# An attention block with normalization and a feed-forward layer: the second softmax's probabilities turned by transfers and 32x32 blocks

## The chip, the cores and the metric

The kernel runs on one core of one Trainium2 chip. The metric is the device time of one execution in microseconds (us), the median of several runs.

## What is computed

Two sequences of 1024 tokens with 256 features pass a normalization with a learned modulation, an attention with **two softmaxes**, and a feed-forward layer. The first softmax, over the first 128 features of queries and keys, gives a context whose tanh corrects the queries of the second.

```python
SCALE = 1.0 / float(np.sqrt(HEAD_DIM))                   # 1/4
qkv = hidden_states @ c_attn_w + c_attn_b
Q, K, V = jnp.split(qkv, 3, axis=2)
attn_scores = jnp.einsum('bse,bte->bst', Q, K) * SCALE
Q_cam, K_cam, V_cam = (Q[:, :, :D_K], K[:, :, :D_K], V[:, :, :D_K])      # D_K = 128
base_A = softmax(jnp.einsum('bsd,btd->bst', Q_cam, K_cam) * SCALE)
layer_weight = sigmoid(cam_w0[0] + cam_w1[0] * LAYER_DEPTH)
cam_ctx = jnp.einsum('bst,btd->bsd', base_A, V_cam)
cam_bias = jnp.einsum('bsd,btd->bst', jnp.tanh(cam_ctx * cam_gate), K_cam)
cam_bias = cam_bias * (SCALE * layer_weight)
final_attn = softmax(attn_scores + cam_bias)
context = jnp.einsum('bst,bte->bse', final_attn, V)
output = context @ c_proj_w + c_proj_b
...
h = _layernorm(x) * (1 + ca) + sa
x = x + ga * attention(h)
h = _layernorm(x) * (1 + cb) + sb
x = x + gb * (gelu(h @ proj1.T + proj1_bias) @ proj2.T + proj2_bias)
```

## The kernel before

`B = 2` batches are worked one after the other. In each the attention is cut into 16 **units** of 128 query tokens: units 0 to 7 are the first softmax's rows, 8 to 15 the second's. Every matrix product is written as three products of a high and a low part (`mm3`, L189 to L191), so each operand is kept as a rounded copy (`_hi`) and the rest (`_lo`).

A batch's attention is a loop of 18 **steps** `s`, written out by hand once for each engine; the engines meet by semaphores. Around the change the engines do this:

- TensorE: `scores(s)` into one of two 1024-wide banks `s_ps`; `transpose_probs(s-2)` (L1157), eight 128x128 transposes of the probabilities `prob` by the identity, into the two 512-wide banks `t_ps`; a filler (projections, or `cam_context` in steps 5, 7, 9 and 11); from step 11 on `attend(s-11)`, which is unit s-3's product with the values, 24 matmuls. After step 17 come `h_transpose` (L1084, the normalized tiles, into `t_ps` too), the last `attend`, and the feed-forward layer.
- VectorE: `row_max(s)` (L790), `prob_low(s-2)` (L784, the low part of the transposed probabilities, read from `t_ps`), `row_recip(s)` (L794), in steps 6, 8, 10, 12 `q_update` (L772 to L778), from step 11 on `attn_gated` (L805, the result times the reciprocal sum and a gate). In step 14 `norm_stats` takes the statistics of the four finished tiles at once, in step 15 `norm_apply` (L739) normalizes them.
- ScalarE: `prob_high(s-2)` (L556, the rounded copy from `t_ps`), `softmax_exp(s)` (L566), and `cam_tanh`.
- GpSimd: the first softmax's division (L369); in batch 0, steps 8 to 15, `split_ffn` (L378, L380, the feed-forward weights' high and low parts, which wait for that step's row maximum); sums with constants and results (L387, L393); `inv_std` (L364), the power -1/2 of the variance, once in step 15.
- SP issues every transfer in one order: inputs, gates, the two feed-forward weights, then the output tiles.

The probabilities of three units fit into `prob`; unit u's exponential waits until unit u-3 is transposed. A bank of `t_ps` is free again when `prob_low` has read it: the list `T_JOBS` gives the order in which the two banks are used, and `read_out` the semaphore that frees one. The loop of steps on TensorE is:

```python
for s in range(UNITS + 2):
    if s < UNITS:
        scores(b, s)
    if s >= 2:
        transpose_probs(b, s - 2)
    ...
    if s >= T + 3:
        attend(b, s - T - 3)
```

## Time and profile before

| | us |
|---|---|
| median of 3 runs | 318.41 |
| lowest and highest run | 317.71, 318.41 |
| the profiled execution, its whole time | 317.94 |
| its span in the profile | 316.1 |
| TensorE busy | 311.3 |
| VectorE busy | 209.8 |
| ScalarE busy | 158.8 |
| GpSimd busy | 107.8 |

The span runs from the first to the last instruction; what lies around it makes up the rest of the execution's time. An engine's busy time is the time in which at least one of its instructions runs; matmuls overlap, so the sum of their lengths is more than TensorE's busy time. The granted TensorE clock is full (tenths of 9 in every slice) throughout. The transfers have moved nearly all their bytes by 62 us; after that the 16 DMA engines are all but idle.

### The profile page before, as it was taken

The page shows a single profiled execution, that of the slowest core. Times are in us where ns is not written, and L with a number is a line of the kernel's source. Part 1 is how long each engine was busy: PE and PEld are TensorE (multiplying, and loading weights), DVE is VectorE, ACT ScalarE, POOL GpSimd, SP SyncE. Part 2 cuts the span into 40 slices and gives each one's busy share as a digit, 9 for nine tenths or more (in the row PEclk, how much of TensorE's full clock was granted, in tenths as well). Part 3 has the DMA queues.
Part 4 walks back from the last instruction along what each step waited for, and adds up shares of the span by engine and source line. Part 5 has one row for each costly group of instructions (what it writes and reads, how often), then busy time and mean ns, then how long its engine had stood idle before and what let it go on. Part 6 is the DMA issues. An engine that isn't in the chain of part 4 may idle for free.

```text
span 316.1 us, 5217 instructions
## 1 busy us (share of the span) xinstructions
PE 311.3 (98%) x2016; PEld 283.0 (90%) x2016; DVE 209.8 (66%) x415; ACT 158.8 (50%) x268; POOL 107.8 (34%) x131
## 2 busy tenths in 40 slices
PE   8999999999999999999999999999999999999996
PEld 6888988989998998998899988889999999899895
DVE  4875888869475769768734698886754675852531
ACT  2775756445322447709902577544522244950930
POOL 4517653244465548035020141230013233503311
PEclk9999999999999999999999999999999999999999
DMA  7920200700000000010000000000000000001001
GB/s 229 350 88 1 66 3 8 260 0 2 1 0 2 0 2 1 2 50 17 3 33 33 2 1 2 0 0 2 2 0 0 2 0 2 0 3 51 17 14 56
DMA packets 8025, 10.31 MB, mean 33 GB/s; under 512 B 704, under 2 KB 6592, under 8 KB 8000
## 3 DMA queue, kind: packets, MB, share of 16 engines
q1 hardware_dynamic: 8000, 9.98, 9.7%
q8 instruction: 16, 0.26, 0.3%
q14 instruction: 9, 0.07, 0.1%
HBM read 7.35 MB, written 2.10 MB: 30 GB/s over the span
## 4 chain that ended last, share of the span: by engine, by line
PE 96%; DMA 2%; SPq 1%; DVE 0%; issue 0%; ACT 0%; DVEq 0%
PE a_ps L191 15%; PE a_ps L189 15%; PE a_ps L190 15%; PE s_ps L189 12%; PE s_ps L191 12%; PE s_ps L190 12%; PE t_ps L1157 9%; PE t_ps L1084 2%; DMA wp_raw<-wp 2%; PE a_ps L1066 1%; PE s_ps L1015 1%; PE s_ps L1019 1%; PE s_ps L1024 1%; PE t_ps L960 1%; PE a_ps L979 1%; PE a_ps L1075 0%
## 5 line engine op out<-in xcount | busy, mean ns | idle before, releaser
L556 ACT ACTIVATE pt_hi<-t_ps 128x512 fp32r<-128x512 f32 x64 | 34.8, 596 | 70.0 <-PE t_ps L1157 69.9
L790 DVE TENSOR_REDUCE nmax<-s_ps 128x1 f32<-128x1024 f32 x32 | 39.0, 1220 | 22.9 <-PE s_ps L191 22.8
L566 ACT ACTIVATE prob<-s_ps,nmax 128x1024 f32<-128x1024 f32 x32 | 35.8, 1119 | 12.9 <-DVE nmax L790 12.7
L784 DVE TENSOR_TENSOR pt_lo<-t_ps,pt_hi 128x512 fp32r<-128x512 f32 x64 | 40.9, 680 | 1.3 <-ACT pt_hi L556 1.3
L189 PE MATMUL s_ps<-k_hi,q_hi 128*128 128x512 f32 x96 | 38.3, 399 | 0.0
L191 PE MATMUL s_ps<-k_hi,q_lo 128*128 128x512 f32 x96 | 37.7, 393 | 0.0
L190 PE MATMUL s_ps<-k_lo,q_hi 128*128 128x512 f32 x96 | 37.5, 391 | 0.0
L189 PE MATMUL a_ps<-v_hi,pt_hi 128*128 128x256 f32 x128 | 36.8, 288 | 0.0
L189 PE MATMUL a_ps<-w_hi,pt_hi 128*128 128x256 f32 x128 | 36.4, 284 | 0.0
L190 PE MATMUL a_ps<-w_lo,pt_hi 128*128 128x256 f32 x128 | 36.2, 283 | 0.0
L191 PE MATMUL a_ps<-w_hi,pt_lo 128*128 128x256 f32 x128 | 36.2, 283 | 0.0
L191 PE MATMUL a_ps<-v_hi,pt_lo 128*128 128x256 f32 x128 | 35.8, 279 | 0.0
L190 PE MATMUL a_ps<-v_lo,pt_hi 128*128 128x256 f32 x128 | 35.7, 279 | 0.0
L369 POOL TENSOR_SCALAR prob<-prob,rinv 128x1024 f32<-128x1024 f32 x16 | 18.3, 1146 | 49.7 <-DVE rinv L794 49.6
L1157 PE MATMUL t_ps<-ident,prob 128*128 128x128 f32 x256 | 33.3, 273 | 0.0
L1157 PEld LDWEIGHTS t_ps<-ident,prob 128*128 128x128 f32 x256 | 29.7, 141 | 4.0
L819 DVE TENSOR_TENSOR pt_lo<-prob,pt_hi 128x512 fp32r<-128x512 f32 x32 | 22.9, 729 | 14.0 <-ACT pt_hi L590 13.7
L393 POOL TENSOR_TENSOR x_all<-x_all,o 128x256 f32<-128x256 f32 x16 | 11.8, 738 | 54.7 <-DVE o L805 54.7
L277 POOL TENSOR_TENSOR x_all<-x_all,o 128x256 f32<-128x256 f32 x15 | 11.4, 760 | 52.7 <-DVE o L814 52.7
L587 ACT ACTIVATE prob<-s_ps,cols_sb 128x512 f32<-128x512 f32 x32 | 22.1, 691 | 13.6 <-PE s_ps L191 13.5
L189 PE MATMUL s_ps<-ht_hi,w_hi 128*128 128x512 f32 x64 | 25.2, 394 | 0.0
L191 PE MATMUL s_ps<-ht_hi,w_lo 128*128 128x512 f32 x64 | 24.9, 390 | 0.0
(156 smaller groups left out, 756.1 us busy)
## 6 DMA issues: line engine op xcount, KB each, us to landing
w_raw<-w_t SPq DMA_DIRECT2D x2, 1024.0 KB, 6.3
out<-x_all SPq DMA_DIRECT2D x16, 128.0 KB, 1.7
x_all<-x SPq DMA_DIRECT2D x4, 256.0 KB, 4.7
wmod_raw<-wmod SPq DMA_DIRECT2D x1, 1024.0 KB, 8.3
x_all<-x SPq DMA_DIRECT2D x2, 512.0 KB, 10.4
wmod_raw<-wmod SPq DMA_DIRECT2D x1, 512.0 KB, 4.5
wattn_raw<-w_attn SPq DMA_DIRECT2D x1, 512.0 KB, 5.5
gates<-h SPq DMA_DIRECT2D x4, 128.0 KB, 2.4
```

The lines of the kernel that those rows point to most:

```text
L189: nc.tensor.matmul(o, st_hi, mv_hi, start=first, stop=False)
L190: nc.tensor.matmul(o, st_hi, mv_lo, start=False, stop=False)
L191: return nc.tensor.matmul(o, st_lo, mv_hi, start=False, stop=last)
L369: G.tensor_scalar(prob[:, u % 3, :], prob[:, u % 3, :], rinv[:, u:u + 1], 1.0, ALU.mult, ALU.mult).then_inc(pnorm_ready, 1)
L393: G.tensor_tensor(xt, xt, o1[:, t % 2, :], ALU.add).then_inc(x2_ready, 1)
L556: A(pt_hi[:, (u // 2) % 2, 4 * g:4 * g + 4, (u % 2) * P:(u % 2 + 1) * P], t_bank(b, "p", 2 * u + g)[:, :].rearrange("p (t n) -> p t n", n= ...
L566: A(prob[:, u % 3, :], s_ps[u % 2][:, :], ACT.Exp, bias=nmax[:, u:u + 1], accum_out=rsum[:, u:u + 1]).then_inc(exp_ready, 1)
L587: A(gelu_of(n), s_bank(n % 4), ACT.Gelu, bias=cols_sb[:, C_B1 + n % HC:C_B1 + n % HC + 1]).then_inc(gelu_ready, 1)
L784: V.tensor_tensor(pt_lo[dst], t_bank(b, "p", 2 * u + g)[:, :].rearrange("p (t n) -> p t n", n=P), f(pt_hi[dst]), ALU.subtract).then_inc(pt ...
L790: V.tensor_reduce(nmax[:, u:u + 1], s_ps[u % 2][:, :], AX.X, ALU.max, negate=True).then_inc(nmax_ready, 1)
L819: V.tensor_tensor(gt_lo[:, n % HC, :], gelu_of(n), f(gt_hi[:, n % HC, :]), ALU.subtract)\
L1157: last = nc.tensor.transpose(t_bank(b, "p", 2 * u + g)[:, t * P:(t + 1) * P], prob[:, u % 3, c:c + P], ident[:, :])
```

## The change

Units 8 to 13 of each batch (`DMA_UNITS`) are no longer transposed by TensorE. ScalarE writes their exponentials with the columns rearranged (four groups of eight runs of 32). SP copies the unit to device memory (`turned`) in four transfers of 128 KB, one for each 32 partitions, waits for them and reads the whole unit back as 128 rows of 4 KB into `quad`, a view of `f32s`, which grows from three to four buffers. In this layout the 128x128 transposition is left to do only inside 32x32 blocks, and VectorE does that with two instructions of 128x512 into `t_ps`. Units 14 and 15 and the first softmax stay as they were. Beside this, other work is put in another order: ScalarE's exponential of steps 10 to 14 stands ahead of the rounding of the turned unit; VectorE's reciprocals and statistics, the row maximum of step 15 and the normalization move, as does GpSimd's `inv_std`.

```diff
--- before.py
+++ after.py
@@ -20,6 +20,8 @@
 DEPTH = 0.5
 NV = DK + E
 UNITS = 2 * T
+Q = P // 32
+DMA_UNITS = range(T, UNITS - 2)
 C_CT, C_BQ, C_BK, C_BVC, C_BV, C_GATE, C_B1, C_W0, C_W1 = 0, 4, 6, 8, 9, 11, 12, 20, 21
@@ -65,7 +67,7 @@
-        f32s = sb("f32s", [P, 3, HALF])
+        f32s = sb("f32s", [P, 4, HALF])
...
+        turned = nc.dram_tensor("turned", (B * len(DMA_UNITS), Q, 32, Q, S // Q), F32, kind="Internal").ap()
+        quad = f32s[:, :, :].rearrange("p (d g) n -> p d (g n)", g=2)
...
@@ -178,6 +183,8 @@
+        probs_out = sem("probs_out")
+        probs_back = [sem(f"probs_back{d}") for d in range(2)]
...
@@ -314,7 +325,28 @@
             wait(sp, qk_psum, 0, 8)
             sp.dma_start(w1_raw[:, :, :], w1_t.rearrange("(c p) n -> p c n", p=P)).then_inc(w1_in, 16)
             sp.dma_start(w2_raw[:, :, :], w2_t.rearrange("(c p) n -> p c n", p=P)).then_inc(w2_in, 16)
+            def write_probs(b, u):
+
+                wait(sp, exp_ready, b, u + 1)
+                for i in range(Q):
+                    sp.dma_start(turned[dma_unit(b, u), :, :, i, :].rearrange("q c n -> c q n"),
+                                 prob[32 * i:32 * (i + 1), u % 3, :].rearrange("p (q n) -> p q n", q=Q))\
+                        .then_inc(probs_out, 16)
+
+            def read_probs(b, u):
+
+                sp.wait_ge(probs_out, 16 * Q * (dma_unit(b, u) + 1))
+                if u - 2 in DMA_UNITS:
+                    wait(sp, t_psum, b, 2 * (u - 2) + 2)
+                else:
+                    wait(sp, qklo_ready, b, 8)
+                sp.dma_start(quad[:, u % 2, :], turned[dma_unit(b, u), :, :, :, :].rearrange("q c i n -> (q c) (i n)"))\
+                    .then_inc(probs_back[u % 2], 16)
+
             for b in range(B):
+                for u in DMA_UNITS:
+                    write_probs(b, u)
+                    read_probs(b, u)
                 for t in range(T):
                     wait(sp, y_ready, b, t + 1)
                     sp.dma_start(out_v[:, b * T + t, :], x_all[:, b * T + t, :]).then_inc(y_out, 16)
@@ -453,12 +485,12 @@
                     if b == 0 and s >= T:
                         wait(pool, nmax_ready, b, s + 1)
                         split_ffn(s - T)
-                    if s == UNITS - 1:
-                        inv_std(b, 2)
                     if s >= 10:
                         attn_const(b, s - 10)
                     if s >= 11:
                         attn_residual(b, s - 11)
+                    if s == UNITS - 1:
+                        inv_std(b, 2)
                 attn_const(b, 6)
                 attn_residual(b, 5)
                 attn_const(b, 7)
@@ -561,10 +593,14 @@
                 wait(act, nmax_ready, b, u + 1)
                 if b and u < 3:
                     wait(act, glo_ready, b - 1, 2 * HC)
-                if u >= 3:
+                if u - 3 in DMA_UNITS:
+                    act.wait_ge(probs_out, 16 * Q * (dma_unit(b, u - 3) + 1))
+                elif u >= 3:
                     wait(act, t_psum, b, 2 * (u - 2))
-                A(prob[:, u % 3, :], s_ps[u % 2][:, :], ACT.Exp, bias=nmax[:, u:u + 1],
-                  accum_out=rsum[:, u:u + 1]).then_inc(exp_ready, 1)
+                dst, src = prob[:, u % 3, :], s_ps[u % 2][:, :]
+                if u in DMA_UNITS:
+                    dst, src = dst.rearrange("p (q t r) -> p t q r", q=Q, t=T), src.rearrange("p (t q r) -> p t q r", q=Q, t=T)
+                A(dst, src, ACT.Exp, bias=nmax[:, u:u + 1], accum_out=rsum[:, u:u + 1]).then_inc(exp_ready, 1)
             def cam_tanh(b, p):
@@ -623,12 +659,15 @@
                         qk_bias(b, j)
                         v_high(b, j - 1)
                 for s in range(UNITS + 2):
+                    if s - 2 in DMA_UNITS and s < UNITS - 1:
+                        softmax_exp(b, s)
                     if s >= 2:
                         prob_high(b, s - 2)
                     if s < 2 and b + s:
                         v_high(b, 3 + s)
+                    if s < UNITS and (s - 2 not in DMA_UNITS or s == UNITS - 1):
+                        softmax_exp(b, s)
                     if s < UNITS:
-                        softmax_exp(b, s)
                         for kind, k in fillers(b, s):
                             if kind == "v" and s >= 2:
                                 v_high(b, k)
@@ -720,6 +759,19 @@
                         wait(dve, x2_ready, b, t + 1)
                     last = V.bn_stats(bst[:, t, :], x_all[:, b * T + t, :])
                 last.then_inc(bst_ready[n // 2], 1)
+                norm_moments(b, n)
+
+            def tile_stats(b, t):
+
+                wait(dve, x2_ready, b, t + 1)
+                last = V.bn_stats(bst[:, t, :], x_all[:, b * T + t, :])
+                if t == TH - 1:
+                    last.then_inc(bst_ready[1], 1)
+                    norm_moments(b, 2)
+
+            def norm_moments(b, n):
+
+                h = n % 2
                 wait(dve, bst_ready[n // 2], b, n % 2 + 1)
                 for t in range(h * TH, (h + 1) * TH):
                     last = V.bn_aggr(mv[:, t, :], bst[:, t, :])
@@ -776,6 +828,16 @@
                 V.tensor_copy(q_hi[dst], t).then_inc(qphi_ready, 1)
                 wait(dve, qphi_ready, b, p + 1)
                 V.tensor_tensor(q_lo[dst], t, f(q_hi[dst]), ALU.subtract).then_inc(qplo_ready, 1)
+
+            def turn_probs(b, u):
+
+                dve.wait_ge(probs_back[u % 2], 16 * (b * len(DMA_UNITS[u % 2::2]) + (u - DMA_UNITS.start) // 2 + 1))
+                for g in range(2):
+                    if (w := read_out(T_JOBS, T_READ_OUT, (b, "p", 2 * u + g))) is not None:
+                        dve.wait_ge(*w)
+                    V.transpose(t_bank(b, "p", 2 * u + g)[:, :].rearrange("p (a i c) -> p i a c", a=TH, i=Q),
+                                quad[:, u % 2, :].rearrange("p (i g a r) -> p g i a r", i=Q, g=2, a=TH)[:, g, :, :, :])\
+                        .then_inc(t_psum, 1)
             def prob_low(b, u):
                 for g in range(2):
@@ -867,22 +929,33 @@
                         qk_split(b, j)
                         v_low(b, j - 1)
                 for s in range(UNITS + 2):
-                    if s < UNITS:
+                    if s < UNITS - 1:
                         row_max(b, s)
                     if b == 0 and s == 0:
                         qk_low(3)
                     if s < 2 and b + s:
                         v_low(b, 3 + s)
+                    if s - 2 in DMA_UNITS:
+                        turn_probs(b, s - 2)
+                        if s < UNITS - 1:
+                            row_recip(b, s)
+                    if s == UNITS:
+                        attn_gated(b, s - T - 4)
+                        tile_stats(b, TH - 1)
                     if s >= 2:
                         prob_low(b, s - 2)
-                    if s < UNITS:
+                    if s == UNITS - 1:
+                        row_max(b, s)
+                    if s < UNITS - 1 and s - 2 not in DMA_UNITS:
                         row_recip(b, s)
+                    if s == UNITS:
+                        row_recip(b, s - 1)
                     for kind, k in fillers(b, s - 1):
                         if kind == "ctx":
                             q_update(b, k)
-                    if s == UNITS - 1:
+                    if s == UNITS:
                         norm_apply(b, 2)
-                    if s >= T + 3:
+                    if s >= T + 3 and s != UNITS - 1:
                         attn_gated(b, s - T - 3)
                     if s < UNITS:
                         for kind, k in fillers(b, s):
@@ -898,8 +971,8 @@
                                 dve.wait_ge(row_psum, 1)
                                 V.tensor_tensor(consts[:, 0, 0, :], a_bank(0, "row", 0)[:, 0:E], consts[:, 0, 0, :],
                                                 ALU.add).then_inc(row_added, 1)
-                    if s == UNITS - 2:
-                        norm_stats(b, 2)
+                    if UNITS - TH <= s < UNITS - 1:
+                        tile_stats(b, s - UNITS + TH)
                 h_split(b, 4)
                 h_split(b, 5)
                 attn_gated(b, T - 1)
@@ -1227,7 +1300,7 @@
                 for s in range(UNITS + 2):
                     if s < UNITS:
                         scores(b, s)
-                    if s >= 2:
+                    if s >= 2 and s - 2 not in DMA_UNITS:
                         transpose_probs(b, s - 2)
                     if s < UNITS:
                         for kind, k in fillers(b, s):
```

TensorE's queue has 96 transposes fewer. How the queues stand around the places where the others meet it:

VectorE, batch 0, step 11 and the next row maximum (`s_ps` are the scores' banks, `t_ps` the turned probabilities', `f32s` the buffer read back), before:

```order
L790 TENSOR_REDUCE nmax<-s_ps 128x1
L784 TENSOR_TENSOR pt_lo<-t_ps,pt_hi 128x4x128 x2
L794 RECIPROCAL rinv<-rsum 128x1
L805 SCALAR_TENSOR_TENSOR o<-a_ps,rinv,gates 128x256
L790 TENSOR_REDUCE nmax<-s_ps 128x1
```

and now:

```order
L852 TENSOR_REDUCE nmax<-s_ps 128x1
L838 STREAM_TRANSPOSE t_ps<-f32s 128x4x4x32 x2
L856 RECIPROCAL rinv<-rsum 128x1
L846 TENSOR_TENSOR pt_lo<-t_ps,pt_hi 128x4x128 x2
L867 SCALAR_TENSOR_TENSOR o<-a_ps,rinv,gates 128x256
L852 TENSOR_REDUCE nmax<-s_ps 128x1
```

The two block transposes stand behind the row maximum, and the reciprocal, which waits for the exponential, ahead of the low part.

VectorE, batch 0, steps 15 and 16, before:

```order
L790 TENSOR_REDUCE nmax<-s_ps 128x1
L784 TENSOR_TENSOR pt_lo<-t_ps,pt_hi 128x4x128 x2
L794 RECIPROCAL rinv<-rsum 128x1
L739 TENSOR_SCALAR xn<-x_all,mv,rstd 128x256 x4
L805 SCALAR_TENSOR_TENSOR o<-a_ps,rinv,gates 128x256
L784 TENSOR_TENSOR pt_lo<-t_ps,pt_hi 128x4x128 x2
L805 SCALAR_TENSOR_TENSOR o<-a_ps,rinv,gates 128x256
```

and now:

```order
L838 STREAM_TRANSPOSE t_ps<-f32s 128x4x4x32 x2
L846 TENSOR_TENSOR pt_lo<-t_ps,pt_hi 128x4x128 x2
L852 TENSOR_REDUCE nmax<-s_ps 128x1
L867 SCALAR_TENSOR_TENSOR o<-a_ps,rinv,gates 128x256
L767 BN_STATS bst<-x_all 128x6
L777 BN_AGGR mv<-bst 128x2 x4
L780 TENSOR_SCALAR ve<-mv 128x4
L846 TENSOR_TENSOR pt_lo<-t_ps,pt_hi 128x4x128 x2
L856 RECIPROCAL rinv<-rsum 128x1
L791 TENSOR_SCALAR xn<-x_all,mv,rstd 128x256 x4
L867 SCALAR_TENSOR_TENSOR o<-a_ps,rinv,gates 128x256
```

Unit 13's block transposes and low part come ahead of the last row maximum; the last tile's statistics and the normalization stand a step later.

SP, from the gates on, before:

```order
L312 DMA gates<-h 64x512 x4
L315 DMA w_raw<-w_t 128x2x1024
L316 DMA w_raw<-w_t 128x8x256
L320 DMA out<-x_all 128x256 x16
L35 UNCONDITIONAL_BRANCH
```

and now, up to the second unit of six:

```order
L323 DMA gates<-h 64x512 x4
L326 DMA w_raw<-w_t 128x2x1024
L327 DMA w_raw<-w_t 128x8x256
L332 DMA turned<-prob 32x4x256 x4
L343 DMA f32s<-turned 128x1024
L332 DMA turned<-prob 32x4x256 x4
L343 DMA f32s<-turned 128x1024
```

Five transfers a unit stand between the weights and the output tiles of the batch.

## Rows read from the trace of the kernel before

**Rows 1.** The page: busy time of each engine, and the chain by engine

```profile
PE 311.3 (98%) x2016; PEld 283.0 (90%) x2016; DVE 209.8 (66%) x415; ACT 158.8 (50%) x268; POOL 107.8 (34%) x131
...
PE 96%; DMA 2%; SPq 1%; DVE 0%; issue 0%; ACT 0%; DVEq 0%
```

**Rows 2.** The chain that ended last, in order of time: start, us

```profile
84.24 0.87 PE t_ps L1157 x8
```

**Rows 3.** The page's groups: busy, mean ns of one | idle before

```profile
L1157 PE MATMUL t_ps<-ident,prob 128*128 128x128 f32 x256 | 33.3, 273 | 0.0
```

**Rows 4.** Timeline of TensorE: start us, us, engine, line, op

```profile
90.52 1.04 PE L1157 MATMUL t_ps<-ident,prob 128*128 128x128 f32 x8
...
96.96 1.04 PE L1157 MATMUL t_ps<-ident,prob 128*128 128x128 f32 x8
...
114.71 1.03 PE L1084 MATMUL t_ps<-ident,xn 128*128 128x128 f32 x8
```

**Rows 5.** Timeline of SP: issue of the feed-forward weights' two loads

```profile
53.91 0.37 SPq L315 DMA_DIRECT2D w_raw<-w_t  x1
54.33 0.47 SPq L316 DMA_DIRECT2D w_raw<-w_t  x1
```

**Rows 6.** The page's DMA issues: count, KB each, median us to landing

```profile
out<-x_all SPq DMA_DIRECT2D x16, 128.0 KB, 1.7
...
wattn_raw<-w_attn SPq DMA_DIRECT2D x1, 512.0 KB, 5.5
gates<-h SPq DMA_DIRECT2D x4, 128.0 KB, 2.4
```

**Rows 7.** The tile w_raw: landings of its two loads

```profile
DMA to landing us min/median/max: 4.9/6.3/7.6
```

**Rows 8.** The page's groups: VectorE's low part of the turned probabilities

```profile
L784 DVE TENSOR_TENSOR pt_lo<-t_ps,pt_hi 128x512 fp32r<-128x512 f32 x64 | 40.9, 680 | 1.3 <-ACT pt_hi L556 1.3
```

**Rows 9.** Timeline of VectorE, batch 0

```profile
71.57 1.23 DVE L790 TENSOR_REDUCE nmax<-s_ps 128x1 f32<-128x1024 f32 x1 [2.57 <-PE s_ps L191]
...
76.73 1.22 DVE L790 TENSOR_REDUCE nmax<-s_ps 128x1 f32<-128x1024 f32 x1
...
87.00 0.88 DVE L772 SCALAR_TENSOR_TENSOR th<-th,lw_scaled,q_lo 128x256 f32<-128x256 f32 x1
...
89.47 0.48 DVE L805 SCALAR_TENSOR_TENSOR o<-a_ps,rinv,gates 128x256 f32<-128x256 f32 x1
...
101.26 1.40 DVE L721 BATCH_NORM_STATS2 bst<-x_all 128x6 f32<-128x256 f32 x4
...
117.68 0.69 DVE L751 TENSOR_TENSOR ht_lo<-h,ht_hi 128x512 fp32r<-128x512 f32 x1
```

**Rows 10.** Timeline of ScalarE, batch 0

```profile
63.00 1.12 ACT L566 ACTIVATE prob<-s_ps,nmax 128x1024 f32<-128x1024 f32 x1
...
77.99 1.12 ACT L566 ACTIVATE prob<-s_ps,nmax 128x1024 f32<-128x1024 f32 x1 [1.27 <-DVE nmax L790]
...
79.09 0.56 ACT L574 ACTIVATE th<-a_ps,gate_bias,cols_sb 128x256 f32<-128x256 f32 x1
...
91.15 1.09 ACT L556 ACTIVATE pt_hi<-t_ps 128x512 fp32r<-128x512 f32 x2 [4.26 <-PE t_ps L1157]
```

**Rows 11.** Timeline of VectorE, batch 1: the query update

```profile
235.80 0.47 DVE L772 SCALAR_TENSOR_TENSOR th<-th,lw_scaled,q_lo 128x256 f32<-128x256 f32 x1
...
237.44 0.48 DVE L805 SCALAR_TENSOR_TENSOR o<-a_ps,rinv,gates 128x256 f32<-128x256 f32 x1
```

**Rows 12.** Timeline of GpSimd, batch 0, step 15

```profile
104.91 0.62 POOL L378 TENSOR_SCALAR w_hi<-w_raw 128x512 fp32r<-128x512 f32 x1 [2.75 <-DVE nmax L790]
105.61 1.29 POOL L380 TENSOR_TENSOR w_lo<-w_raw,w_hi 128x512 fp32r<-128x512 f32 x1
106.86 1.03 POOL L364 TENSOR_TENSOR rstd<-ve,minus_half 128x4 f32<-128x4 f32 x1
107.88 0.74 POOL L387 TENSOR_TENSOR x_all<-x_all,consts 128x256 f32<-128x256 f32 x1
```

More of the change, by code:

```diff
@@ L260, in mod_psum, with dma_unit @@
             return mod_bank(n, c)[:, 0:4 * MOD_N].rearrange("p (v a b) -> p a b v", b=B, v=4)[:, 0, :, :]
+        def dma_unit(b, u):
+            return b * len(DMA_UNITS) + u - DMA_UNITS.start
         def gelu_of(n):
```

## The prediction

> **What bounds the kernel now.** I read the page first. TensorE is busy for 311.3 of 316.1 us and makes 96% of the chain that ended last; VectorE is busy for 66%, ScalarE for 50%, GpSimd for 34% [rows 1]. So time comes off only where TensorE's instruction stream gets shorter, and the other engines have room as long as none of them makes TensorE wait. Next the chain in order of time: each group of eight block transposes of one unit stands in it with 0.87 us [rows 2], and 12 such groups go. The group's own line has 273 ns for one transpose [rows 3]. That is a length, not a price: eight of them take 1.04 us in the timeline, and they overlap their neighbours [rows 4].
>
> A rule of the Trainium skill sets another price ("TensorE: Matmul & The Clock Gate", Part 4: PE-mode transpose): a transpose costs about 275 ns inside a kernel. The trace agrees on the length and not on the cost: by the page 96 transposes are worth 26.4 us (an estimate), by the chain 10.4.
>
> **What is removed.** 12 groups x 0.87 = 10.4 us, 5.2 for each batch, all on the path. They come back only if each unit reaches TensorE in time by the new way, so I follow it. Units 0 to 7 are the first softmax, 8 to 15 the second; step s computes the scores of unit s, turns unit s-2 and attends with unit s-3. A step from 12 on is now 6.44 us (90.52 to 96.96, [rows 4]) and becomes 5.57.
>
> **What is added on the DMA queue.** Each unit needs four writes of 128 KB and one read of 512 KB. SP issues about every 0.45 us (53.91, 54.33 [rows 5]), so the last write leaves 1.4 us after the first. A 128 KB store of the same 1 KB rows lands in 1.7 us, a 128 KB copy in 2.4 [rows 6]: write 3.1 to 3.8, I take 3.5. For the read: two loads of 1 MB issued 0.42 apart landed after 4.9 and 7.6 us [rows 7], so the second MB cost 3.1 us more, and 512 KB should take 4.9 - 1.55 = 3.4; the ends are 2.4 (128 KB) and 5.5 (512 KB in the crowded start [rows 6]). With 0.2 for two handovers the **round trip** is 7.1 us, between 5.5 and 11 (5.5 twice). SP does these in order and is free again before the next exponential, which comes over 4.5 us later; the two weight loads ahead of them have landed by 62.
>
> **What is added on VectorE.** Two transposes of 128x512 in 32x32 blocks per unit, 24 in all. None is in the trace. The nearest row by size and by its use of t_ps is the subtraction of 128x512, 680 ns [rows 8]; I take 0.65 from start to start (two run in 1.28 to 1.29). The bounds are 0.6 (half of the 1.22 us of a row maximum over 1024, 76.73 [rows 9]) and twice the row, 1.36, for a form that needs two passes. From the start of a step's row maximum (call it m) the exponential starts at 1.26 (76.73, 77.99 [rows 10]), and the next ScalarE work 1.10 later (79.09), so the rounding of the turned unit starts at m+2.36 and its second half 0.5 later. The two block transposes run from m+1.14 to m+2.45, beside the exponential: they are **hidden up to 0.85 us each**. The low parts follow at about m+3.0 and m+3.6, so the unit is ready for TensorE at m+4.25 and VectorE free at m+4.2. Behind that stand the gated output (0.40), one tile's statistics (1.40/4 = 0.35 [rows 9]) and, in steps 10 and 12, the query update: 2.47 in batch 0 (87.00 to 89.47 [rows 9]), 1.64 in batch 1 (235.80 to 237.44 [rows 11]).
>
> **Batch 0, by hand.** TensorE without a wait: attention of unit 9, 10, 11, 12 could start at 82.3, 87.9, 93.5, 99.05 (the old start of the transposes of that step less 0.87 for each group gone before). Row maxima: step 10 at 71.57 [rows 9]; step 11 at 71.57+4.2+2.47 = 78.2; step 12 when its scores are there, or VectorE free (78.2+4.6): 82.8; step 13 at 82.8+4.2+2.47+0.75 = 90.2; step 14 at 95.15; the transposes of unit 13, which step 15 does first, at 100.1. Units 9 to 12 are ready at 82.45, 87.05, 94.45, 99.4. TensorE waits 0.15 for unit 9 and 0.85 for unit 11: 1.0 us. In step 15 the row maximum comes behind unit 13's work, at 102.65. On GpSimd a weight split waits for it (0.62 + 1.29, [rows 12]), then two sums of 0.74, and only then the inverse deviation (1.03), which the change moved to the end: 108.3. VectorE's normalization waits for that, and the low part of unit 15 is queued behind it; TensorE's transposes of the normalized tiles need that bank. They are done near 111.9 against 115.6 (114.71 [rows 4] and one group's 0.87). Batch 0 gains **3.7 us**, of 5.2.
>
> **Batch 1.** The query update is 0.83 shorter twice and there is no weight split, so by the same steps each unit is ready when TensorE gets there: **5.1 us**. The feed-forward layers follow the transposes of the normalized tiles by the same steps as now (114.71 [rows 4], the last low part at 117.68 [rows 9]) and cost nothing. The exponential's permuted output keeps runs of 32 elements; ScalarE writes 128x512 with runs of 128 in half of 1.09 [rows 10], and I take no change.
>
> **The transfers' deadline.** Unit 8: exponential over at 63.00+1.12 [rows 10], wanted at 71.57+1.14: 8.6 us. Units 9 to 12 have 10 to 11. Unit 13 is tightest: over at 90.2+2.36, wanted at 100.1, 7.5 us; the same in batch 1. 7.1 fits, barely.
>
> **Sum:** 3.7 + 5.1 = 8.8 us. The profiled execution took 317.94 us (span 316.1), so 309.1; the median of the runs is 0.47 above it: **309.6 us**.
>
> **Rivals.**
> *A longer round trip.* For: the margin is 0.4 us and only a start-up row has this size. Against: the queue is empty then. At 9 us unit 13 is 1.5 late in each batch, nearly all of which TensorE waits, and unit 8 0.4 in batch 0: 3.4 us, 313. Each us more costs about 3.8; from 10.5 the gain is gone. The skill speaks for this side ("DMA: Bandwidth & Descriptors", Anatomy of one DMA): most of a transfer's fixed time is the receipt of its last write, longest towards HBM. The trace's 1.7 us for a store includes it.
> *VectorE becomes the bound: slower.* Place: VectorE's queue in steps 10 to 15. At 1.07 us a transpose each step is 0.35 longer, unit 13 some 2.2 to 2.5 later, and 5 us remain: 313.5. From **1.25 us** it decides against the change; at 1.36 each step is 0.95 longer, unit 13 5.7 to 6.2 later against 3.7 + 5.1 gained, and the time is 321. Against: every single-pass row of this size is below 0.9. The skill's "VectorE: DVE Perf Modes", The three transpose paths, gives 311 ns for a VectorE transpose of 128x128 bf16; if all of it grew with the columns, 512 would be 1.24 (an estimate), at the turning point, and its table of rules keeps 128x128 transposes on TensorE. No row here shows the operation.
> *No wait at all,* with 10.4 back: 308.0, within the forecast's own range. That TensorE keeps the work is excluded: its queue has 96 transposes fewer.
>
> **How the numbers follow.** Forecast 0.58 (own range 307.8 to 311.5). Longer round trip, still faster, 0.20. Mild VectorE bound 0.09. Slower by VectorE 0.06, by the round trip 0.03. Within 0.3% (about 1 us, what measuring this kernel can tell from no change) 0.04. So faster 0.87, same 0.04, slower 0.09. The range 307.7 to 315 leaves out the slow cases, the no-change case and the far end of the round trip.
>
> **What would show it.** Right: 160 transposes of the probabilities left on TensorE; the span of steps 12 to 14 near 5.6 us each; the block transposes 0.6 to 0.85 us; the last of a unit's transfers landed within 7.5 us of its exponential; TensorE waits of about 1.5 us in batch 0, around units 9, 11 and 15. Wrong: VectorE idle before the block transposes with a DMA as releaser (first rival), or block transposes over 0.85 us with steps over 5.6 (second). The forecast fails altogether if VectorE's ops next to the transfers, or the matmuls themselves, run longer than before.

## The result, and the profile after

The changed kernel takes **309.0 us** (median of four runs, 308.48 to 309.38), the kernel before 318.13 us in the same session: a ratio of 0.970, 95% interval 0.965 to 0.975. The profiled execution took 309.08 us with a span of 307.3, against 317.94 and 316.1. The forecast was 309.6.

The page, with its busy times, the DMA row of the 40 slices, the chain by engine, a group of part 5 and the issues of part 6:

```profile
span 307.3 us, 5121 instructions
...
PE 300.9 (98%) x1920; PEld 273.1 (89%) x1920; DVE 223.4 (73%) x439; ACT 158.7 (52%) x268; POOL 107.4 (35%) x131
...
DMA  7920200736655000010011000004656400001001
...
PE 86%; DVE 5%; DMA 2%; ACT 2%; issue 2%; SPq 1%; POOL 1%; DVEq 0%; POOLq 0%
...
L846 DVE TENSOR_TENSOR pt_lo<-t_ps,pt_hi 128x512 fp32r<-128x512 f32 x64 | 41.1, 683 | 3.8 <-ACT pt_hi L588 3.7
...
turned<-prob SPq DMA_DIRECT2D x48, 128.0 KB, 2.9
f32s<-turned SPq DMA_DIRECT2D x12, 512.0 KB, 3.6
```

TensorE is 10.4 us less busy than in [rows 1] and has 96 matmuls fewer. VectorE has 13.6 us more, ScalarE and GpSimd what they had. The DMA engines, idle in the second softmax before, are some 30 to 60% busy there (digits 3 to 6). TensorE's share of the chain fell from 96% to 86%: the chain now leaves it in places.

The new operation and the transfer it reads from, in the view of the tile `f32s`:

```profile
L838 DVE STREAM_TRANSPOSE t_ps<-f32s x24: 683/697/718, 73.2 to 244.6; 128x512 f32<-128x512 f32 x24
...
DMA to landing us min/median/max: 3.1/3.6/4.7
```

TensorE's timeline: the first scores of batch 0, the scores of units 12 to 15, then the transposes of the normalized tiles in batches 0 and 1.

```profile
24.75 0.59 PE L196 MATMUL s_ps<-k_hi,q_hi 128*128 128x512 f32 x1
...
80.26 0.40 PE L196 MATMUL s_ps<-k_hi,q_hi 128*128 128x512 f32 x1
...
85.81 0.40 PE L196 MATMUL s_ps<-k_hi,q_hi 128*128 128x512 f32 x1
...
91.37 0.40 PE L196 MATMUL s_ps<-k_hi,q_hi 128*128 128x512 f32 x1
...
97.00 0.40 PE L196 MATMUL s_ps<-k_hi,q_hi 128*128 128x512 f32 x1
...
110.80 1.23 PE L1157 MATMUL t_ps<-ident,xn 128*128 128x128 f32 x8 [0.61 <-DVE pt_lo L846]
...
254.43 1.03 PE L1157 MATMUL t_ps<-ident,xn 128*128 128x128 f32 x8
```

Steps 12, 13 and 14 take 5.55, 5.56 and 5.63 us, against 6.44 [rows 4]. The rows also give two **stretches** that I use below, because the kernel's start varies from one execution to the next: the first scores come at 24.2 in one profile and at 26.1 in another, where the granted clock was also 0.64 from 8 to 12 us. Stretch 0 runs from the first scores to the transposes of the normalized tiles in batch 0, stretch 1 from there to the same group of batch 1. Before they were 90.49 and 148.61 us (24.22 to 114.71 to 263.32), now they are 86.05 and 143.63. So batch 0 gained 4.4 and batch 1 5.0; a start 0.5 us later hides a part of it in the span.

VectorE's timeline, step 12 of batch 0 and what follows up to the normalization:

```profile
83.19 1.23 DVE L852 TENSOR_REDUCE nmax<-s_ps 128x1 f32<-128x1024 f32 x1 [0.61 <-PE s_ps L198]
84.33 1.31 DVE L838 STREAM_TRANSPOSE t_ps<-f32s 128x512 f32<-128x512 f32 x2
85.69 0.16 DVE L856 RECIPROCAL rinv<-rsum 128x1 f32<-128x1 f32 x1
86.18 1.29 DVE L846 TENSOR_TENSOR pt_lo<-t_ps,pt_hi 128x512 fp32r<-128x512 f32 x2 [0.33 <-ACT pt_hi L588]
87.38 0.48 DVE L824 SCALAR_TENSOR_TENSOR th<-th,lw_scaled,q_lo 128x256 f32<-128x256 f32 x1
...
89.03 0.48 DVE L867 SCALAR_TENSOR_TENSOR o<-a_ps,rinv,gates 128x256 f32<-128x256 f32 x1
...
99.55 1.30 DVE L838 STREAM_TRANSPOSE t_ps<-f32s 128x512 f32<-128x512 f32 x2
...
102.13 1.22 DVE L852 TENSOR_REDUCE nmax<-s_ps 128x1 f32<-128x1024 f32 x1
...
107.87 1.80 DVE L791 TENSOR_SCALAR xn<-x_all,mv,rstd 128x256 f32<-128x256 f32 x4 [1.14 <-POOL rstd L396]
```

The block transposes run back to back behind the row maximum and wait for no transfer. The same step on ScalarE:

```profile
84.45 1.11 ACT L603 ACTIVATE prob<-s_ps,nmax 128x1024 f32<-128x1024 f32 x1 [2.64 <-DVE nmax L852]
...
85.56 1.08 ACT L588 ACTIVATE pt_hi<-t_ps 128x512 fp32r<-128x512 f32 x2
```

The exponential covers the block transposes, and the rounding starts the moment it ends. SP's queue for units 12 and 13 of batch 0 (x4 are the four writes, the row behind is the read):

```profile
85.68 1.94 SPq L332 DMA_DIRECT2D turned<-prob  x4
89.85 0.34 SPq L343 DMA_DIRECT2D f32s<-turned  x1
92.23 1.75 SPq L332 DMA_DIRECT2D turned<-prob  x4
95.94 0.34 SPq L343 DMA_DIRECT2D f32s<-turned  x1
```

From the first write to the read pass 4.17 and 3.71 us. Unit 13, the tightest, is read from 95.94 and turned at 99.55, with no wait recorded before it.

### The profile page after: what moved, and what is told of

The parts are those of the page before. It is cut to its first block, busy times and chain, and to the rows that moved or that the text cites. A ratio compares the mean times of both kernels' runs of the same rounds, so it can differ in the third digit from the quotient of the medians.

```text
span 307.3 us, 5121 instructions
## 1 busy us (share of the span) xinstructions
PE 300.9 (98%) x1920; PEld 273.1 (89%) x1920; DVE 223.4 (73%) x439; ACT 158.7 (52%) x268; POOL 107.4 (35%) x131
## 4 chain that ended last, share of the span: by engine, by line
PE 86%; DVE 5%; DMA 2%; ACT 2%; issue 2%; SPq 1%; POOL 1%; DVEq 0%; POOLq 0%
PE a_ps L196 13%; PE a_ps L198 13%; PE a_ps L197 13%; PE s_ps L196 12%; PE s_ps L198 12%; PE s_ps L197 12%; PE t_ps L1230 5%; PE t_ps L1157 2%; DMA wp_raw<-wp 2%; DVE nmax L852 2%; DVE pt_lo L846 1%; ACT prob L603 1%; ACT pt_hi L588 1%; PE a_ps L1139 1%; PE s_ps L1088 1%
## 5 line engine op out<-in xcount | busy, mean ns | idle before, releaser
L623 ACT ACTIVATE prob<-s_ps,cols_sb 128x512 f32<-128x512 f32 x32 | 22.1, 690 | 13.6 <-PE s_ps L198 13.5
L197 PE MATMUL s_ps<-ht_lo,w_hi 128*128 128x512 f32 x64 | 24.9, 390 | 0.0
L197 PEld LDWEIGHTS a_ps<-w_lo,pt_hi 128*128 128x128 f32 x128 | 24.6, 192 | 0.2
```

The costliest lines, as they stand in the source:

```text
L197: nc.tensor.matmul(o, st_hi, mv_lo, start=False, stop=False)
L623: A(gelu_of(n), s_bank(n % 4), ACT.Gelu, bias=cols_sb[:, C_B1 + n % HC:C_B1 + n % HC + 1]).then_inc(gelu_ready, 1)
```

## The experiments

My theory: the gain is the chain's 0.87 us for each of 12 groups, and all that was added lies beside other work, as long as one block transpose stays under 0.85 us and the round trip under some 7.5. The rivals: the new order of the queues brings the gain; the transfers cost something; VectorE costs something. All runs in one table (medians in us, ratio to the kernel before on the same chip with its 95% interval, stretches from each profile):

| kernel | time | ratio | stretch 0 | stretch 1 |
|---|---|---|---|---|
| before | 318.1 | | 90.49 | 148.61 |
| changed | 309.0 | 0.970 (0.965 to 0.975) | 86.05 | 143.63 |
| order alone | 318.14 | 1.000 (0.997 to 1.003) | 90.33 | 148.63 |
| no transfers | 308.95 | 0.970 (0.965 to 0.976) | 86.06 | 143.65 |
| no transfers, small transposes | 308.45 | 0.970 (0.963 to 0.976) | 85.56 | 143.60 |
| turned twice | 316.59 | 0.995 (0.992 to 0.998) | 90.11 | 147.43 |
| exponential behind | 320.32 | 1.006 (1.003 to 1.008) | 91.74 | 149.12 |
| four units | 311.41 | 0.981 (0.978 to 0.983) | 86.96 | 145.24 |
| seven units | 311.15 | 0.979 (0.976 to 0.981) | 86.66 | 144.78 |
| inverse deviation first | 308.21 | 0.969 (0.968 to 0.971) | 85.64 | 143.64 |
| read later | 332.93 | 1.049 (1.043 to 1.056) | 96.21 | 156.80 |
| SP waits for the read | 326.14 | 1.023 (1.017 to 1.029) | 93.82 | 152.51 |
| a second read ahead | 333.18 | 1.045 (1.039 to 1.052) | 98.29 | 156.13 |
| a small read ahead | 313.59 | 0.986 (0.985 to 0.988) | 87.87 | 146.11 |

### Where the gain comes from

**Order alone.** No unit goes the new way; of the new order only the work of steps 14 to 16 and the statistics (VectorE) and `inv_std` (GpSimd) stay. The places of ScalarE's exponential and of VectorE's reciprocal in steps 10 to 14 are tied to `DMA_UNITS` in the code, so with an empty range both are as before.

```diff
-DMA_UNITS = range(T, UNITS - 2)
+DMA_UNITS = range(T, T)
```

> The kernel with the new order of VectorE's and GpSimd's work in steps 15 and 16 and the statistics tile by tile, but with all units transposed by TensorE (no transfers, no block transposes). If the gain is the 12 removed groups, the order alone gives nothing or costs a little at the end of each batch: 318 to 319.5 us. If part of the 9 us came from the order, this run is faster than before: 316 or less.

318.14, and both stretches within 0.16 us of before. This part of the order brings nothing by itself. The rest was not run alone, but it had nothing to give back: in the kernel before TensorE waits for VectorE twice in all, 1.2 us at the start and 0.2 us for `v_lo`, and never in steps 10 to 16.

**No transfers.** SP's loop over `DMA_UNITS` and the waits on the transfers are gone, and one more memset at the start fills the new buffer.

```diff
             for b in range(B):
-                for u in DMA_UNITS:
-                    write_probs(b, u)
-                    read_probs(b, u)
...
-                if u - 3 in DMA_UNITS:
-                    act.wait_ge(probs_out, 16 * Q * (dma_unit(b, u - 3) + 1))
-                elif u >= 3:
+                if u >= 3:
```

> The changed kernel without its 60 transfers and the waits for them; the block transposes read what the buffer happens to hold, so the second softmax's probabilities of units 8 to 13 are left out of the result. If the transfers are hidden, as forecast, nothing moves: 309.0 us, within 0.5. If their lateness or the traffic beside the other engines costs, the time falls: by 0.5 to 2 us, to 307 to 308.5.

The stretches agree with the changed kernel's to 0.02 us. Six MB written and six read back cost nothing where they stand.

**Small transposes.** The same, and each block transpose takes 32 columns in place of 512.

```diff
+                    V.transpose(t_bank(b, "p", 2 * u + g)[:, 0:32], quad[:, u % 2, 32 * g:32 * g + 32]).then_inc(t_psum, 1)
```

> No transfers as in the run before, and each block transpose shrunk from 128x512 to 128x32, so the result is wrong in the second softmax. If the block transposes are hidden beside the exponential in steps 10 to 14, only step 15, where no exponential covers them, gets shorter: about 1 us at the end of batch 0 and nothing in batch 1, 308 us. If VectorE's load is what keeps the last 1.3 us of the 10.4 from showing, 306 to 307.

Stretch 0 is 0.5 us shorter, stretch 1 the same. Block transposes of 15.7 us in all (12 pairs of 1.31) became 3.7 (12 of 0.31), and gave at most 0.5 us back.

**Four units** in place of six (units 12 and 13 stay on TensorE).

```diff
-DMA_UNITS = range(T, UNITS - 2)
+DMA_UNITS = range(T, UNITS - 4)
```

> Only units 8 to 11 go by transfers. Four groups of 0.87 us come back to TensorE: 3.5 us more, 312.5. If the end of a batch (the late row maximum behind unit 13) is what costs in batch 0, up to 1 us less than that: 311.5.

311.41, the second of the two values expected. Four groups of 0.87 make 3.48 for each batch; the stretches gain 3.53 and 3.37. The first four units bring their full price; the last two bring 0.91 of 1.74 in batch 0 and 1.61 in batch 1. What was lost of the 5.2 is lost at the batch's end: TensorE's wait of 0.61 before the normalized tiles is there with six units and not with four.

### How close the other engines are

**Turned twice.** Each block transpose is done once into `xn`, idle at that time, and then again.

```diff
+                    src = quad[:, u % 2, :].rearrange("p (i g a r) -> p g i a r", i=Q, g=2, a=TH)[:, g, :, :, :]
+                    V.transpose(xn[:, :, :].rearrange("p t e -> p (t e)")[:, g * HALF:(g + 1) * HALF].rearrange("p (a i c) -> p i a c", a=TH, i=Q), src)
```

> Each block transpose is done twice, the first time into an idle buffer, so a unit costs VectorE 2.6 us more or less instead of 1.3. By the forecast's steps a unit is then ready about 0.9 us later in its step, VectorE needs 6.0 us a step against TensorE's 5.57, and the gain is nearly gone: 316 to 319 us. If VectorE has more room than that, 311 to 313.

316.59. Its waits (us in total, times, longest):

```profile
PE a_ps L196 <- DVE pt_lo L848: 3.4, 4, 1.2
PE t_ps L1232 <- DVE pt_lo L848: 2.0, 4, 0.7
```

TensorE now waits eight times for the low parts that stand behind the block transposes, where the changed kernel waits once, for 0.6. At 1.3 us for each transpose 1.5 of the 9.1 us gained are left. So the turning point was not reached at the 1.25 predicted; it should lie a little beyond 1.3 (an estimate, no run has a longer one).

**Exponential behind** the rounding of the turned unit, as in the kernel before.

```diff
-                    if s - 2 in DMA_UNITS and s < UNITS - 1:
-                        softmax_exp(b, s)
...
-                    if s < UNITS and (s - 2 not in DMA_UNITS or s == UNITS - 1):
+                    if s < UNITS:
                         softmax_exp(b, s)
```

> ScalarE's exponential of steps 10 to 14 stands behind the rounding of the turned unit, as before the change. By the forecast's offsets the exponential is then over at m+4.2 instead of m+2.4; VectorE's reciprocal waits for it with the low parts behind it, the unit is ready at m+5.6 instead of 4.25 and VectorE needs 6.35 us a step: 316 to 320. If this order does not matter, 309.

320.32, 0.6% slower than the kernel before. VectorE's timeline in its step 12:

```profile
85.08 1.22 DVE L850 TENSOR_REDUCE nmax<-s_ps 128x1 f32<-128x1024 f32 x1
86.21 1.31 DVE L836 STREAM_TRANSPOSE t_ps<-f32s 128x512 f32<-128x512 f32 x2
89.28 0.16 DVE L854 RECIPROCAL rinv<-rsum 128x1 f32<-128x1 f32 x1 [1.76 <-ACT prob L603]
...
92.91 1.21 DVE L850 TENSOR_REDUCE nmax<-s_ps 128x1 f32<-128x1024 f32 x1
```

ScalarE rounds first and exponentiates after, and VectorE idles 1.76 us at the reciprocal; this step, with its query update, takes 7.83 us, the two beside it 5.9 and 6.2. So the gain exists only with the exponential ahead. What that place is worth without the block transposes was not run.

**Seven units.** Unit 14 goes the new way too, and in step 16 the gated output and the statistics stand ahead of its block transposes.

```diff
-DMA_UNITS = range(T, UNITS - 2)
+DMA_UNITS = range(T, UNITS - 1)
```

> Unit 14 too goes by transfers, with the gated output and the statistics of step 16 ahead of its block transposes. TensorE loses 0.87 us more in each batch, 1.7 in all. If the round trip of 7.5 us fits, 307.3. By the forecast's steps it does not quite: unit 14's exponential is over at 97, it is back at 104.5 and its low part ends 2.5 us later, about when TensorE wants the bank for unit 15, so 309 to 310.5.

Two more groups gone, one in each batch, and still 2.1 us slower than six units, just above the range expected. TensorE comes to unit 15's transposes and finds their bank not free:

```profile
PE t_ps L1230 <- DVE pt_lo L846: 3.4, 2, 2.0
```

Neither VectorE nor the transfers have room there. VectorE comes to unit 14's block transposes at 104.85 in batch 0, behind the gated output and the statistics; the unit's read was issued at 101.04, and a read takes at least 3.2 us here, so a shorter queue would soon have met the transfer.

**Inverse deviation first** in GpSimd's step 15, as it was before the change.

```diff
                     if b == 0 and s >= T:
...
+                    if s == UNITS - 1:
+                        inv_std(b, 2)
                     if s >= 10:
                         attn_const(b, s - 10)
```

> GpSimd's inverse deviation stands ahead of the two sums in step 15 again, as in the kernel before. If TensorE's wait of about 1 us at the end of batch 0 comes from the normalization that waits for GpSimd, the normalization starts 1 us earlier and up to 0.8 us come back, in batch 0 alone: 308.2 to 308.6. If that wait is set by VectorE's own queue, nothing: 309.0.

308.21, and 0.41 us less in stretch 0: what the profiles show of the move's cost. The ratios of the two kernels overlap, so this version is the best by its profile, not by the interval. The inverse deviation is over 1.2 us earlier, but VectorE wins less, since its four instructions of the normalization now run beside three of GpSimd's sums (1.80 us for them in the changed kernel, beside one):

```profile
106.65 2.61 DVE L791 TENSOR_SCALAR xn<-x_all,mv,rstd 128x256 f32<-128x256 f32 x4
```

### How close the transfers are

**Read later.** A read of 64 KB of the unit stands ahead of its full read, and SP waits for it.

```diff
+                sp.dma_start(quad[:, u % 2, 0:P], src[:, 0:P]).then_inc(probs_back[u % 2], 16)
+                sp.wait_ge(probs_back[u % 2], 16 * (2 * n + 1))
+                sp.dma_start(quad[:, u % 2, :], src).then_inc(probs_back[u % 2], 16)
```

> Each unit's read waits for one more small read of 64 KB, so the round trip grows by some 2.4 us to about 10 us. By the forecast's deadlines (7.5 us for unit 13, 8.6 for unit 8) unit 13 comes some 2.3 us late in each batch and unit 8 over 1 us: 314 to 316 us, with VectorE idle before the block transposes of units 8 and 13 alone. If the path has more slack than that, under 311.

332.93: a **miss** by 17 us beyond the range. Latency alone would have made units 8 and 13 late. The waits say that all twelve are:

```profile
DVE t_ps L841 <- DMA f32s<-turned: 27.6, 12, 3.7
```

and SP's timeline suggests why: from one unit's first write to the next pass 7.1 to 7.3 us (70.25, 77.56, 84.64; 6.0 to 8.6 over both batches), more than a step of 5.56. SP does each unit's writes, wait, read and wait in series. It falls behind by some 1.6 us per unit, and the lateness adds up. My theory had only a deadline and lacked this rate. The next run tests it without any transfer added.

**SP waits for the read.** SP waits until a unit is back before it begins the next.

```diff
                 sp.dma_start(quad[:, u % 2, :], turned[dma_unit(b, u), :, :, :, :].rearrange("q c i n -> (q c) (i n)"))\
                     .then_inc(probs_back[u % 2], 16)
+                sp.wait_ge(probs_back[u % 2], 16 * (b * len(DMA_UNITS[u % 2::2]) + (u - DMA_UNITS.start) // 2 + 1))
```

> No transfer is added or made longer: SP only waits, after each unit's read, until it has landed, before it goes on to the next unit's writes. If SP's queue is the hidden second limit (what it does for one unit, one after the other, must fit into a step of 5.57 us), a unit takes it 3.7 us up to the read and 3.7 us more until it has landed, 7.4 in all; the steps 10 to 14 then take 7.4 us instead of 5.6, and five such steps in each batch give 309 + 18 = 327 us, 323 to 330. If only the round trip against each unit's deadline counts, as the forecast's first rival had it, the round trip of a unit is as before and the time stays at 309 to 310.

326.14. Neither the bytes nor a unit's own round trip grew; the read even lands sooner (median 3.2 us, at most 3.4). SP's timeline:

```profile
79.18 2.36 SPq L332 DMA_DIRECT2D turned<-prob  x4
83.48 0.34 SPq L343 DMA_DIRECT2D f32s<-turned  x1
86.72 1.75 SPq L332 DMA_DIRECT2D turned<-prob  x4
90.44 0.34 SPq L343 DMA_DIRECT2D f32s<-turned  x1
93.69 1.75 SPq L332 DMA_DIRECT2D turned<-prob  x4
```

A round of 6.9 to 7.5 us, from one unit's first write to the next, sets the pace: five rounds a batch, each some 1.5 us over the step, are 15 us, near the 17 lost. The queue's serial round is a limit of its own.

The same trace charges a long wait twice. TensorE's row at the end of batch 0's second softmax, and windows of 3 us around it (busy time of PE, PEld, DVE, ACT and POOL, PEclk, DMA share, GB/s):

```profile
109.93 1.94 PE L1231 MATMUL t_ps<-ident,prob 128*128 128x128 f32 x8 [3.48 <-DVE pt_lo L847]
...
107.00:110.00 3.00, 0.07 (x1) 0.10 (x2) 2.23 (x4) 1.19 (x2) 0.00 (x0) 0.91 0.02 8
110.00:113.00 3.00, 3.00 (x15) 3.00 (x16) 2.93 (x9) 1.46 (x3) 1.32 (x2) 0.52 0.03 8
113.00:116.00 3.00, 3.00 (x28) 3.00 (x27) 1.88 (x4) 1.06 (x3) 3.00 (x5) 1.00 0.00 0
```

TensorE idles for 3.48 us, until unit 13's low part has freed a bank, and then works at a granted clock of 0.52, about its lower level of 1.2 GHz, for the next 3. The eight transposes take 1.94 us there, for 1.04 at the full clock. That is some 1.4 us (0.48 of 3) on top of the wait, and the same happens at the end of batch 1 (a wait of 3.62, then 0.59 for 3 us): some 3 of the 17 us lost. In the changed kernel TensorE's longest wait in these steps is 0.61 us, and its mean clock was 0.998. The clock also falls now and then without such waits: one execution of the kernel before had a mean of 0.989 and took 321.48 us for 318.1; the cause of that stays open.

**A second read ahead.** Each unit is read twice: first into `xn`, which nobody uses then, and behind it, on the same queue, as before. SP waits only for the spare read of the unit before, and VectorE for the last spare read before it normalizes into `xn`.

```diff
+                if dma_unit(b, u):
+                    sp.wait_ge(spare_back, 16 * dma_unit(b, u))
+                sp.dma_start(xn[:, :, :].rearrange("p t e -> p (t e)"), turned[dma_unit(b, u), :, :, :, :].rearrange("q c i n -> (q c) (i n)"))\
+                    .then_inc(spare_back, 16)
```

> Each unit's read is issued right behind a second read of the same 512 KB into an idle buffer. SP is busy for 0.35 us more, but the unit is back about 1.9 us later (0.35 for the issue, 1.55 for the bytes at the rate of the weight loads). If the deadlines count (7.5 us for unit 13, 8.6 for unit 8, 10 for the others), unit 13 is up to 1.9 us late in each batch and the others hardly: 311 to 313. If SP's queue alone counts, its round grows to about 4.1 us, still under a step: 309 to 310.

333.18: a **miss** for all that I had written down. The spare read delays the needed one by only some 2 us (landing 5.5 us, median). But the next unit's writes are issued right behind both reads:

```profile
68.36 0.43 SPq L348 DMA_DIRECT2D f32s<-turned  x1
68.83 2.04 SPq L333 DMA_DIRECT2D turned<-prob  x4
75.33 0.34 SPq L346 DMA_DIRECT2D xn<-turned  x1
75.71 0.43 SPq L348 DMA_DIRECT2D f32s<-turned  x1
76.19 1.96 SPq L333 DMA_DIRECT2D turned<-prob  x4
```

From first issue to the next read these writes take 6.5 us (6.4 to 7.9 for all behind a unit's reads) in place of some 4, and the round is 7.4 us. Either the bytes do it or the extra issue and wait. The last run tells them apart.

**A small read ahead:** the same with 64 KB for the spare read.

```diff
-                sp.dma_start(xn[:, :, :].rearrange("p t e -> p (t e)"), turned[dma_unit(b, u), :, :, :, :].rearrange("q c i n -> (q c) (i n)"))\
+                sp.dma_start(xn[:, :, :].rearrange("p t e -> p (t e)")[:, 0:P], turned[dma_unit(b, u), :, :, :, :].rearrange("q c i n -> (q c) (i n)")[:, 0:P])\
```

> The kernel that reads each unit twice took 333.2 us against 309.0. This one issues the same extra transfer at the same place with the same waits, but of 64 KB (128 rows of 512 bytes) in place of 512 KB. If the loss came from the bytes, which the next unit's writes stand behind on the DMA engines, it is nearly gone: 309 to 311 us, and the four writes land again within 3.7 to 4.4 us of the first issue. If it came from the extra issue and wait in SP's queue, whatever the size, the time stays above 325 us.

313.59, 2.6 us above the range for bytes and far below 325. Some 20 of the 24 us lost were bytes; the other 4.6 are the extra transfer with its 64 KB, more than I expected. Its writes take 4.7 to 5.0 us (once 5.8) and a round 5.6 to 6.7, just over a step, so lateness builds up slowly. VectorE waits for a transfer at four units of batch 1, and in batch 0 only at unit 13:

```profile
101.09 1.32 DVE L843 STREAM_TRANSPOSE t_ps<-f32s 128x512 f32<-128x512 f32 x2 [1.71 <-DMA f32s<-turned]
```

The changed kernel itself has this overlap in mild form. Where a unit's writes are issued right behind the read of the one before, they take longer. SP, batch 1:

```profile
212.90 0.34 SPq L343 DMA_DIRECT2D f32s<-turned  x1
213.38 1.88 SPq L332 DMA_DIRECT2D turned<-prob  x4
219.19 0.34 SPq L343 DMA_DIRECT2D f32s<-turned  x1
```

5.8 us for these writes, the longest of the twelve, against 3.7 for unit 8 of both batches and unit 13 of batch 0, which stand behind no read just issued. Not all of the spread is this: in the run in which SP waits for the read no read is in flight, and nine writes took 3.7 us but three 4.0 to 4.3. The Trainium skill ("DMA: Bandwidth & Descriptors", Queues, rings and completion order) says that each DMA engine takes its descriptors in ring order; the last two runs agree, with some 6.5 and 4.8 us for the same writes behind 1 MB and 576 KB of reads.

## Why the prediction was right

- **What bounds, and what is removed.** 12 groups at 0.87 us of chain [rows 2]: 10.4. TensorE's busy time fell by 10.4 and the steps to 5.55 to 5.63, against 5.57. The rule of the Trainium skill ("TensorE: Matmul & The Clock Gate", Part 4: PE-mode transpose) would have given 26.4 us: the trace agrees with its 275 ns as a length (273 [rows 3], though that figure is for bf16 and these are float32), but the price in a full stream is 0.11 us.
- **Block transposes.** 0.65 from start to start, two in 1.29: measured 1.30 to 1.31 for two, 697 ns for one. The row it was read from, the subtraction of the same 128x512 [rows 8], was the right neighbour, and the 1.24 us that the second rival worked out was nearly twice the measured time. The step's offsets from the row maximum were 1.26 for the exponential and 2.36 for the rounding: measured 1.26 and 2.37.
- **Round trip.** Predicted 3.5 for the write, 3.4 for the read. Measured 3.7 for three of the twelve units' writes, 3.9 to 5.8 for the others, and 3.6 for the read. The term was right for the read and short for the write: it left out that the previous unit's read runs beside it. That cost nothing, since VectorE waits for no transfer in either batch. But the sign of being right, landed within 7.5 us of the exponential, does not hold for every unit: unit 9 of batch 1 needed 5.8 us for the writes and at least 3.1 for the read. Its deadline of 10 to 11 us had room for that. The first rival's sentence on the write receipt was written of transfers by GpSimd's path, while these go by SP; no run shows how much of the 1.7 us is receipt.
- **Batch 0: 3.7 forecast, 4.4 measured.** The mis-sized term is the query update. I took 2.47 us, its length in batch 0 of the kernel before [rows 9]; it ran 1.65 (87.38 to 89.03), the length of batch 1 [rows 11]. GpSimd's weight split and sum, which ran beside it before, are now over at 87.2. So unit 11 was not late, and the 0.85 us of wait for it and 0.15 for unit 9 are absent; only the end's wait of 0.61 is there, about the 0.5 that the forecast had for it (5.2 less 3.7 and 1.0). So one of the signs named, TensorE's waits of 1.5 us around units 9, 11 and 15, did not come. The row maximum of step 15 came at 102.13, for 102.65; as the scores of this execution began 0.53 later, it was 1.0 us early.
- **Batch 1:** 5.1 forecast, 5.0 measured.
- **The sum:** 8.8 forecast for the span, and 316.1 - 307.3 = 8.8. Part of that agreement is luck: the stretches gained 9.4, and the start of that execution was 0.5 us late.
- **Rivals.** VectorE as the bound is borne out by the doubled transposes, with the turning point a little above the 1.25 us stated. The longer round trip was the right worry with the wrong price: "Each us more costs about 3.8; from 10.5 the gain is gone". That counted latency alone. With SP's round lengthened to 7.0 us and more the runs lost 17 to 24 us, because a round over 5.56 makes every unit later than the last. The prediction had seen that SP works in order, and that with its own 3.5 us it is free before the next exponential, but did not carry this into the price of a longer trip. A read that takes longer while SP does not wait for it was not tested, so the 3.8 may hold for that case. The range's upper end of 315 would not have held the loss in SP's round, and the chance of 0.03 rested on a margin that I never worked out: the step of 5.56 against a round of 4.2 to 6.3 (the writes' 3.7 to 5.8 and 0.48 for the read's issue), which stays below it only on average.

## What to carry to other kernels

Price what comes off a saturated engine by its place in the chain (0.87 us for eight), not by the length of an instruction (273 ns each), and price what is added elsewhere by whether its offset within the step still leaves the unit ready; the order that makes room for it can decide the whole gain (320.3 us with the exponential behind, 309.0 with it ahead). A transfer there and back in a pipeline has two conditions, and both must be worked out: its latency against the deadline, and the issuing queue's full round for one unit (issues, waits, and the bytes that stand ahead on the same DMA engines) against the step. Missing the second costs at every step, as the runs show; missing the first should cost once for each late unit, which no run shows by itself.

## What the hardware showed that I had not expected

- A block transpose of 128x512 in float32 from SBUF to PSUM takes VectorE 683 to 718 ns, about what its subtraction of that size takes (683).
- Four writes of 128 KB in rows of 1 KB need mostly 3.7 us from the first issue until SP goes on when alone, some 4.8 behind reads of 576 KB, 6.5 behind 1 MB.
- VectorE's work ran slower beside GpSimd's: the first two instructions of the query update took 0.88 and 0.85 us beside GpSimd's weight split and sum and 0.48 and 0.43 behind them; the four instructions of the normalization 2.61 beside three sums, 1.80 beside one and 1.37 in batch 1 with GpSimd idle but for the first 0.12. This was read from the traces and not tested apart. The Trainium skill has the rule ("SBUF — State Buffer", Who interferes with whom): an instruction of VectorE with two inputs in SBUF contends with one of GpSimd that reads SBUF. The trace agrees for the query update, whose first two instructions have two inputs in SBUF; the normalization's have one such tensor, so this sentence does not cover them. The rule would have corrected my 2.47 us, had I asked where GpSimd's sum would stand after the change.
- After a wait of 3.5 us TensorE's granted clock was 0.52 for the next 3 us, so that the wait cost about 5 (3.5 and 0.48 of 3).
